# Shared network moved behind the routing front, ahead of the expert tiles; the front as a four-stage pipeline

## The reference

```python
h = _layernorm(x) * (1 + ca) + sa
x = x + ga * mamba(h)            # 4 layers of a Mamba-2 mixer, final rmsnorm
h = _layernorm(x) * (1 + cb) + sb
x = x + gb * ffn(h)
```

```python
normed = h * rsqrt(mean(h*h) + 1e-8) * norm_weight
shared = relu(normed @ sw1 + sb1) @ sw2 + sb2          # 128 -> 512 -> 128
probs  = sigmoid(normed @ router_w.T)
scores, idx = top_k(probs, 2);  w = scores / (sum(scores) + 1e-6)
eo     = relu(normed @ ew1[e] + eb1[e]) @ ew2[e] + eb2[e]
out    = shared + sum over the two experts of w * eo
```

## Time and profile before

| what | value |
|---|---|
| median of 3 runs | 1205.0 us (1202.86 to 1207.61) |
| time of the profiled execution | 1208.51 us |
| span of its trace | 1206.3 us |
| mean granted TensorE clock | 0.953 |
| PE, DVE, ACT, POOL busy | 88%, 83%, 74%, 49% |
| mixer steps | to 856 us |
| front with the shared network | rank of batch 0 at 858.6 us, last slot at 988.6 us |
| first tile | 1007.8 us |

### The profile page before, as it was taken

One profiled execution on the slowest core, in us unless ns is written; L12 is line 12 of the kernel. 1 busy time (PEld: TensorE's weight loads), 2 busy tenths in 40 slices (PEclk: granted clock), 3 DMA queues, 4 the chain that ended last, 5 costly groups with the idle time before them and its releaser, 6 DMA issues.

```text
span 1206.3 us, 27505 instructions
## 1 busy us (share of the span) xinstructions
PE 1062.2 (88%) x7160; PEld 607.1 (50%) x7160; DVE 1001.7 (83%) x1856; ACT 889.9 (74%) x1724; POOL 590.7 (49%) x729
## 2 busy tenths in 40 slices
PE   5799999999999999999999999996778876999970
PEld 4345554455445554455445544543344544777750
DVE  6788999999998999888988899894578885888855
ACT  5688889888888889888888888885466643655530
POOL 0254566545664566435543454334145451666664
PEclk9799999999999999999999999998888987999995
DMA  4111332233222322210000100000010015677637
GB/s 136 35 32 36 131 101 85 83 104 131 83 85 85 137 97 83 74 32 20 24 22 23 28 21 21 24 14 1 3 33 32 29 39 162 224 230 227 217 100 209
DMA packets 85580, 98.07 MB, mean 81 GB/s; under 512 B 20698, under 2 KB 65888, under 8 KB 85536
## 3 DMA queue, kind: packets, MB, share of 16 engines
q1 hardware_dynamic: 80544, 89.08, 23.3%
q0 software_dynamic: 4992, 8.48, 2.1%
HBM read 59.67 MB, written 37.83 MB: 81 GB/s over the span
## 4 chain that ended last, share of the span: by engine, by line
PE 53%; DVE 19%; issue 13%; ACT 7%; DMA 3%; DVEq 2%; POOL 2%; SPq 1%; ACTq 0%; POOLq 0%
PE bank L475 9%; PE bank L548 5%; ACT xbc L1062 4%; DVE cv L1331 3%; PE bank L604 3%; PE bank L522 3%; PE bank L667 3%; PE bank L484 2%; DVE cv L1327 2%; PE bank L485 2%; PE bank L491 2%; PE bank L492 2%; DVE stmp L1434 2%; PE bank L668 2%; PE bank L669 2%
## 5 line engine op out<-in xcount | busy, mean ns | idle before, releaser
L1331 DVE SCALAR_TENSOR_TENSOR cv<-bank,PAR,cv 128x511 f32<-128x511 f32 (+2 forms) x384 | 273.7, 741 | 10.1 <-DVE cv L1327 4.3
L1635 POOL TENSOR_TENSOR yt<-yt,ti 128x384 f32<-128x384 f32 x64 | 64.3, 1004 | 334.5 <-DVE ti L1453 334.5
L1341 DVE TENSOR_TENSOR M<-E,bank 128x512 f32<-128x512 f32 x256 | 170.6, 677 | 42.3 <-PE bank L548 34.3
L929 ACT ACTIVATE E<-bank 128x512 f32<-128x512 f32 x256 | 148.5, 593 | 30.2 <-DVE M L1341 29.0
L475 PE MATMUL bank<-hn,WA 128*128 128x512 f32 x256 | 144.4, 647 | 19.3 <-DVE cv L1331 18.9
L1666 POOL DMA_INDIRECT RS<-y,XR x92 | 99.5, 1082 | 78.3 <-DVE y L1546 56.6
L1079 ACT ACTIVATE hr<-bank,W1B 128x512 f32<-128x512 f32 x92 | 63.3, 688 | 57.4 <-PE bank L669 53.6
L1659 POOL DMA_INDIRECT XS<-stage,IDX x64 | 65.7, 1026 | 76.3 <-DVE run L1306 54.2
L1062 ACT ACTIVATE xbc<-cv 128x512 f32<-128x512 f32 x128 | 77.0, 626 | 21.6 <-DVE yt L1448 20.4
L548 PE MATMUL bank<-M,dtx 128*32 128x128 f32 x2048 | 82.9, 279 | 9.9 <-DVE M L1341 7.3
L1639 POOL TENSOR_TENSOR y<-yt,zs 128x512 f32<-128x512 f32 x64 | 81.4, 1271 | 20.6 <-POOL yt L1635 19.9
(11 more groups left out here) (242 smaller groups left out, 2667.4 us busy)
## 6 DMA issues: line engine op xcount, KB each, us to landing
XS<-PADT SPq DMA_DIRECT2D x32, 520.0 KB, 4.0
WA<-w_in SPq DMA_DIRECT2D x192, 64.0 KB, 1.8
W1B<-WD SPq DMA_DIRECT2D x23, 514.0 KB, 3.6
W2B<-WD SPq DMA_DIRECT2D x23, 512.5 KB, 5.1
WD<-WS SPq DMA_DIRECT2D x16, 512.0 KB, 2.7
XR<-XS SPq DMA_DIRECT2D x23, 260.0 KB, 4.5
RW<-w_in SPq DMA_DIRECT2D x18, 256.0 KB, 4.3
WO_raw<-w_out SPq DMA_DIRECT2D x32, 128.0 KB, 3.4
```

The costliest lines, as they stand in the source:

```text
L929: f(E[i % 2][:, :], bank[2 + i % 2][:, :], ACT.Exp).then_inc(e_a, 1)
L1331: stt(out=cv[t][:, s:L], in0=src[:, 0:L - s], scalar=PAR[:, bass.ds(cw + 3 - s, 1)], in1=cv[t][:, s:L], op0=ALU.mult, op1=ALU.add).then_in ...
L1341: tt(M[i % 4][:, :].rearrange("p (n t) -> p n t", n=4), E[i % 2][:, :].rearrange("p (n t) -> p n t", n=4), bank[5][:, c * CH:(c + 1) * CH] ...
```

## The change

The front and the networks are now two loops. The front (`front(it)`) handles four batches at once, one stage of each: rank and slot of batch it, `square_m` to `scale` and the logits of it+1, `square_x` to `modulate` of it+2, and `square_h` to the centring product of it+3. Then one loop, `network(q)`, runs q = 0 to 30: 8 shared networks, and the 23 tiles. The mean and its subtraction become one matmul with I - 1/128 (`centring`); `square_x` and `normalise_x` read its result from PSUM. The second operation of `modulate` goes from DVE to ACT. Part C of the last step leaves `body(STEPS + 1)` and is issued in pieces around `front(0)`. `stage` and `IDX` have four buffers (SD). The three operation sets `sqf`, `lnf`, `rf` are one for each norm. `RB` now lies in `xT`. The input of a shared network is split from `h` by `high` and `low` in the network loop. On SP, the first expert weights are loaded ahead of the wait for the scatters.

```diff
+SD = 4
 # PE
-            def mean(n): ... mm(first_bank(n), mean128, xT[n]).then_inc(mean_mm, 1)
+            def centre(n):
+                wait(pe, s1_v, 2 * n + 2)
+                wait(pe, nrm_v, n - 1)
+                mm(x_bank(n)[:, :], centring[:, :], xT[:, n * L:(n + 1) * L], start=True, stop=True).then_inc(xc_mm, 1)
             def logits(n):
                 wait(pe, n_v, n + 1)
+                    wait(pe, rt_v, 20 * n)
...
+            def front(it):
+                if it + 1 < NB:
+                    square_mean_of_m(it + 1)
+                if it + 2 < NB:
+                    variance(it + 2)
+                if it + 3 < NB:
+                    square_mean_of_h(it + 3)
+                if it == 0:
+                    last_square_mean()
+                positions(it)
+                if it + 1 < NB:
+                    logits(it + 1)
+                    turn_tokens(it + 1)
+                if it == 0:
+                    last_project_out()
+                if it + 3 < NB:
+                    centre(it + 3)
+            def turn_base(n):
+                wait(pe, fo_v, n + 1)
+                wait(pe, base_a, n)
+                wait(pe, stage_a, 2 * NB)
...
+            def network(q):
+                i = q - NB
+                for t in range(HT):
+                    if q < NB + NT:
+                        if t == 0:
+                            wait(pe, xh_a, q + 1)
+                            wait(pe, xl_v, q + 1)
...
+                        up(q, t, SW[0] if i < 0 else W1B[i % 2])
+                    if q > 0:
...
+                        down(q - 1, t, SW[1] if i < 1 else W2B[(i - 1) % 2])
+                    if t == 0 and i > 1:
+                        turn_result(i - 2)
+                    if t == 1 and 1 < q < NB + 2:
+                        turn_base(q - 2)
+                    if t == 2 and -1 <= i < NT - 1:
+                        turn_slots(i + 1)
+                    if t == 2 and 2 <= q < 4:
+                        spread_gates(q - 2)
             steps(pe, body)
+            square_mean_of_h(1)
+            logits(0)
+            turn_tokens(0)
+            centre(1)
+            variance(1)
+            square_mean_of_h(2)
+            centre(2)
+            for it in range(NB):
+                front(it)
+            for q in range(NB + NT + 1):
+                network(q)
 # ACT
+            (before the loop) square_h(1) root_h(1) exp_logits(0) square_h(2) put_tokens(0)
+            square_x(1) root_x(1) root_h(2) last_squares() modulate(1)
+            def front(it):   # each while the batch exists
+                square_m(it + 1); square_x(it + 2); square_h(it + 3)
+                root_m(it + 1); root_x(it + 2); root_h(it + 3)
+                if it == 0: last_root()
+                exp_logits(it + 1); modulate(it + 2); put_tokens(it + 1)
+            def network(q):
+                for t in range(HT):
+                    relu(q, t, b1)
+                    if t == 2: high(q + 1)
+                    if t == 2 and 1 < q < NB + 2: keep_base(q - 2)
+                    if t == 3 and 2 <= q < 4: keep_gates(q - 2)
+                if q > 0: result(q - 1, ...)
 # DVE
+            add_mamba(1) normalise_x(1) add_mamba(2)
+            def front(it):
+                rank(it)
+                routing_weight(it)
+                scale(it + 1)
+                normalise_x(it + 2)
+                add_mamba(it + 3)
+                slot(it)
+                if it == 0: last_scale_out()
+            low(0)
+            gates()
+            def network(q):
+                for t in range(HT):
+                    halves(q, t)
+                    if t == 0 and i > 1: weigh(i - 2)
+                    if t == 0 and 1 < q < NB + 2: add_shared(q - 2)
+                    if t == 2: low(q + 1)
+            (map_tiles() stands between network(0) and network(1))
 # SP
+            load_up(0)
+            load_up(1)
+            load_down(0)
             scattered(sp, NB)
             load_slots(0)
-            load_up(0)
             load_slots(1)
-            load_up(1)
-            load_down(0)
```

More of the change, by code:

```diff
@@ L150, in build @@
         scope[0] = ctx
[L151 to L155, removed]
+        stage = [sb(f"stage{i}", 8 * ROW) for i in range(SD)]
         m40, utb = sb("m40", 40, BF16), sb("utb", P, BF16)
@@ new lines, in positions @@
+            def positions(n):
+                wait(pe, setup_v, 4)
+                wait(pe, rt_v, 20 * n + 8)
+                mm(bank[5][:, 32:72], utb[:, :], m40[:, :], start=True, stop=False)
+                for d in range(1, 5):
+                    ins = mm(bank[5][:, 32 + 8 * d:72], onesb[:, :], m40[:, 0:40 - 8 * d], start=False, stop=(d == 4))
+                ins.then_inc(pos_mm, 1)
+            def front(it):
[15 more added lines that the diff above has]
+                    centre(it + 3)
@@ L791, in _ @@
-            turn_base(NB - 1)
-            wait(pe, r_a, HT * NB)
-            wait(pe, dg_v, NB)
-            for g in range(2):
-                mm(bank[g][:, :], ones_row[:, :], DG[:, g * 512:(g + 1) * 512], start=True, stop=True).then_inc(gb_mm, 1)
-            turn_slots(0)
-            for i in range(NT + 1):
-                expert(i)
+            centre(1)
[4 more added lines that the diff above has]
+                front(it)
@@ L911, in root_m @@
-                f(rf[i][:, :], lnf[i][:, :], ACT.Exp, scale=-0.5).then_inc(s2_a, 1)
-            def halve(n):
-                wait(act, n_v, n + 1)
-                wait(act, u_mm, HT * (n - 1))
-                f(nH[:, (n % 2) * L:(n % 2 + 1) * L], nT[n % 2][:, :], ACT.Copy).then_inc(nh_a, 1)
+                root(s3_a, 3 * n + 2, 2, m_bank(n), eps8, n_v, n)
             def exp_logits(n):
@@ L920, in exp_logits @@
                 wait(act, rt_v, 20 * (n - 1) + 1)
[L921 removed]
+                f(pr[:, :], bank[5][:, 0:32], ACT.Exp, scale=-1.0).then_inc(ex_a, 1)
             def body(k, A, B, C, N):
@@ L1042, in body @@
                     root_m(0)
-                    halve(0)
-                    exp_logits(0)
                 if A:
@@ new lines, in last_squares, with last_root @@
+            def last_squares():
+                for t in range(2):
+                    wait(act, fin_p, 4 * STEPS - 2 + 2 * t)
+                    wait(act, ss_mm, STEPS - 1)
+                    f(sqy[t][:, :], y2[t][:, :], ACT.Square).then_inc(sq_a, 1)
+            def last_root():
+                wait(act, ss_mm, STEPS)
+                wait(act, o_v, STEPS - 1)
+                f(lnY[:, :], bank[7][:, :], ACT.Ln, bias=eps5).then_inc(ry_a, 1)
+                wait(act, ry_a, 2 * STEPS - 1)
+                f(rY[:, :], lnY[:, :], ACT.Exp, scale=-0.5).then_inc(ry_a, 1)
@@ L1148, in _ @@
-            steps(act, body)
-            act.wait_ge(hup, NB + STEPS)
-            put_tokens(0)
-            square_h(2)
-            for n in range(NB):
-                front(n)
-            keep_base(NB - 1)
-            for g in range(2):
-                wait(act, gb_mm, g + 1)
-                f(gbB[:, g * 512:(g + 1) * 512], bank[g][:, :], ACT.Copy).then_inc(gb_a, 1)
-            high_slots(0)
-            for i in range(NT + 1):
-                expert(i)
+                wait(act, xl_v, n + 1)
@@ L1163, in _ @@
+            steps(act, body)
+            square_h(1)
+            root_h(1)
+            exp_logits(0)
+            square_h(2)
+            put_tokens(0)
+            square_x(1)
+            root_x(1)
+            root_h(2)
+            last_squares()
+            modulate(1)
+            for it in range(NB):
+                front(it)
+            act.wait_ge(hup, NB + STEPS)
+            high(0)
+            for q in range(NB + NT + 1):
+                network(q)
         @block.vector
@@ L1387, in body @@
                     apply_decay(1)
-                if B and not A:
-                    centre(0)
                 if A:
@@ L1402, in body @@
                     scale_out()
-                if C and not B:
-                    add_mamba(1)
-                    centre(1)
                 if B and not A:
-                    modulate(0)
+                    normalise_x(0)
                 if A:
```

514 lines of the change are left out of this document (223 added, 291 removed).

## The result

The kernel after takes 1210.38 us (median of 4 runs, 1207.79 to 1211.91), the kernel before 1205.33 in the same rounds: a ratio of 1.0038, 95% interval 1.0020 to 1.0057. So the change costs 3 to 5 us by the medians, 0.4%; that is less than the forecast's own measure of "no change" (6 us), but both intervals lie above 1. The forecast was 0.7%. The execution profiled here is the shortest of its four (1207.79 us, span 1206.0), and that of before stood above its median, so the two spans look alike; the medians do not.

The account below looks back on a forecast made before the run. PE bounds the tiles; slack lies at the steps' end, front and before the tiles. 950.0 + 6.8 + 9.1 + 1.0 + 47.2 = 1014.1, plus 198.5 + 2.1 = 1214.7 us span; median 1213, range 1198 to 1224.

Parts of the forecast that it names:

- too-short passes: In the front, passes near 11.7 us instead of the expected 13.4 would show the prediction wrong.
- The end of the steps: Last mixer operand ready at 839.9 us, then slot 0 ends at about 865 and slot 1 at 880 us.
- The full passes: Front passes 2 to 4 begin at half clock and take 13.4 us each, between bounds of 11.7 and 15.5.
- The `modulate` term: In each front pass, moving half of `modulate` to ACT adds 0.7 us on ACT.
- The last three passes: Front passes 5, 6 and 7 take 11.4, 10.0 and 7.6 us, so the last slot ends at 949 us.
- The centring product: In the front, it removes a DVE subtraction of 0.69 us and adds none.
- The networks: Shared networks: 6.8 us for network 0, 9.1 for 1, 1.0 for clock, 47.2 for 2 to 7, with `turn_base` stalling.
- rival 2: PE's clock stays up and `turn_base` never stalls, eight times 1.03 us less in the networks: time 1193 us, chance 0.14.
- Scatters and loads: Between front and tiles, scatters end at 963 us and SP's three earlier weight loads cost nothing.
- rival 1: PE's clock stays up in the front, passes of 11.7 us, last slot 936.5: time 1201 us, chance 0.20.
- Rival 3: Half clock through the whole front, last slot at 960 us: time 1224 us, chance 0.12.
- Rival 4: The change buys no overlap, as other missed waits leave the time at 1205 us: chance 0.09.

Follow-up runs that it names:

- `after_again`: The changed kernel built and timed a second time, unchanged, against the kernel before: 1208.22 us, ratio 1.0035.
- `mod_dve`: The changed kernel with the second operation of `modulate` back on DVE, behind `normalise_x`: 1209.67 us, ratio 1.0042 to the kernel before.
- `subtract`: The changed kernel with the centring product undone, a mean matmul and a DVE subtraction again: 1216.18 us, ratio 1.0094 to the kernel before.
- `base_late`: The changed kernel with PE's `turn_base` moved behind down 2 and ACT's `keep_base` to block 3: 1202.0 us, ratio 0.9981 to the kernel before.
- `filler`: The changed kernel with 12 unused bf16 matmuls behind the positions of front passes 1 to 7: 1202.79 us, ratio 0.9983 to the kernel before.
- `run_late`: The changed kernel with DVE's copy of `first_slot` to `run` moved behind `add_mamba(2)`: 1207.15 us, ratio 1.0024 to the kernel before.

## Why the prediction was right, and where its terms were not

The direction, the size (0.7% forecast, 0.4% measured) and the mechanism are right; the span forecast of 1214.7 stands against 1206.0 and 1209.9 in two traces. There is luck in the direction. The forecast is 8.4 us above the span before, and its terms were 8.7 us too long for the first trace and 4.8 for the second; most of their errors point the same way. It had named too-short passes as a sign of being wrong, and the three full passes average 12.6 us, midway between its 13.4 and the 11.7 of that sign. What held without luck is the structure: the gap ahead of the tiles goes, the front becomes a chain of latencies that PE begins at half clock, and `turn_base` stalls. Point by point:

- **The end of the steps.** Slot 0 at 865 forecast, 862.85 measured; slot 1 at 880, 876.92. "The last mixer operand is ready at 839.9" was 2 us late, 1.5 of it a fall of the clock in the trace of before that this execution did not have (`after_again` had 839.47); the wait of the copy of `run` behind POOL's queue was missed, 2 us the other way. From the start of `add_mamba(1)` to the end of slot 0 are 20.5 us, and the terms give 21.1; the second centring product took 1.12 us and not 2.0. The mixer steps, held unchanged, were so within what the clock does to them.
- **The full passes.** 13.4 forecast, 12.05, 12.86 and 12.83 measured. The term mis-sized is the three roots, 4.2 us: back to back they start every 1.25 us and end after 3.82. The logits took 1.71 to 1.85 instead of 2.0, and one of the three first means 1.15 instead of 2.0. That the pass begins at half clock and is brought back was right, at 0.73 to 0.78. The `modulate` term was wrong as a price for ACT (`mod_dve`), but my 13.4 held no more than the clock-bound chain beside it.
- **The last three passes.** 11.4, 10.0, 7.6 forecast, 9.48, 8.81, 7.48 measured, 3.2 us in all. This is the largest single error. Pass 5 lacks a root and an `add_mamba` on the path, 1.25 + 1.5, and its logits are at full clock (1.03 us at 914.96), where I took off only 2.0.
- **The centring product** "removes a DVE subtraction and adds none" is true, but not its value: 8 us (`subtract`).
- **The networks.** 64.1 us from first to last `low` forecast, 64.6 measured. In it network 1 was 9.48 instead of 10.1, the slow clock fell on network 2 (9.60 instead of 7.86), and the others were 7.65 to 7.89 instead of 7.86. The stall of `turn_base` held (0.57 to 0.78 us of idle time, forecast 1.03; periods 7.65 to 7.89, forecast 7.86): rival 2, that it is not there, fell, and `base_late` is that rival made real, worth 6.2 us of the 8.2 that I gave it.
- **Scatters and loads.** The last scatter's issue ends at 957.2 us (963 forecast), no wait for the slot loads shows, and the first tile follows network 7 without a gap. Right.
- **The rivals.** With the clock held up (`filler`) the time is 1202.8; rival 1 said 1201. Its mechanism is real, but it needs work that the kernel does not have. Rival 3, half clock throughout, did not come. Rival 4, 1205 us, is outside both intervals, by 3 to 5 us only. The chance of "slower than 1211" was added up wrong: rival 3 and two thirds of the forecast are 0.12 + 0.30 = 0.42, not 0.45. The Trainium skill's rule on a swinging clock ("TensorE: Matmul & The Clock Gate", "A second HAM failure mode: psum-queue depth-cycling") agrees in kind with the trace: full and half rate within one pass, worth 5.4 us (`filler`).

So the overlap that the new order gives up shows in five places, each measured by taking it away: the slot at the end of DVE's list (20 us), the transposes ahead of their input (6), the clock in PE's idle time (5, not beside the first), the map in one piece (3), and a copy behind POOL's queue (about 1, not clear of noise).

That the medians differ by 5 us while two single traces have one span is not fully resolved: the trace of `after_again` has 1.6 us of it at the end of the mixer and 2.4 in the front's passes (15.35 instead of 14.07 for the first, 10.16 instead of 9.48 for the fifth), each time with the clock. There is one trace of the kernel before, and why the clock falls at other places in other executions was not tried.

## What to carry to other kernels

When a chain of dependent work is pulled out from under the work that covered it, its latency becomes time: write its loop out, find the one operation that frees the next round, and put it as early in each engine's list as its input allows. The four moves of calls here change no work at all and turn 0.4% slower into 2.2% faster (1.9 to 2.4). A call that waits for another engine (a transpose, a setup copy, a block of bookkeeping) belongs where its input is already there, since it holds everything behind it in its list.

## What the runs showed of the hardware

- **DVE beside POOL.** A DVE operation with both inputs in SBUF can be stretched by a tensor operation on POOL: `add_mamba`'s second, 0.69 us alone, took 1.64 us in `run_late`, and POOL's product 1.59 instead of 1.27; in the kernel after, the 0.42 us comparison at line 1294 took 1.13 beside POOL's addition at 868.78. The operation ahead of it also lies beside POOL (838.55 to 839.34) and took only 0.79 instead of 0.75, so an overlap alone does not give the price. In both stretched cases POOL's operation had begun first and had over 0.8 us left; here only 0.25 us of POOL's addition (837.80 to 838.80) were left, and the product began behind. The Trainium skill says this of the engine ("GPSIMD Engine Reference", "Specifications": SBUF interfaces shared with VectorE, with contention for instructions with two SBUF inputs), and the trace agrees.
- **ACT's small chains.** Six Ln and Exp of 512 columns in a row (895.74 to 899.56 us in the pass shown) take 3.82 us, a little less than the sum of their listed durations, 3.92: they overlap, and a gap between them, as I had added one for each root, is not to be counted.
- **Idle PE costs twice.** In passes 2 to 4 PE was idle for 4.6 us, and the logits then took 1.71 to 1.85 us instead of 1.03, the centring product behind them 1.9 instead of 1.02; twelve matmuls that compute nothing gave back 1.8 us of a pass of 12.8. In pass 5, behind 4.24 us of idle time, the logits still took 1.03 us and the fall came with the centring product (1.92 at 916.68).
